# Scores of a token tile in two blocks, a new order of all queues and a paired maximum, in a six-layer windowed-attention kernel

## The reference

```python
x = attn_layer(shift_tokens(x), Wqkv[i], q_scale[i], k_scale[i], Wo[i]) + x
x = ffn_layer(shift_tokens(x), ln_g[i], ln_b[i], W1[i], b1[i], W2[i], b2[i]) + x
```

## Time and profile before

| | |
|---|---|
| median of 3 runs | 3304.71 us (3296.84 to 3305.41) |
| profiled execution | 3304.44 us, its span 3302.6 us |
| mean granted clock of TensorE | 0.991 of full |
| busy: PE, DVE, ACT, POOL | 94%, 85%, 83%, 78% |
| costliest group of DVE: sums of squares (L1153), 128x1024 to 16 | 384 of 1207 ns |
| DMA, mean | 68 GB/s |
| first output projection of a deep instance begins | 406 us |

### The profile page before, as it was taken

The page is one execution under the profiler, slowest core; times in us unless marked ns, Lnnn a source line. Parts: engine busy times, 40 slices in busy tenths (PEclk is TensorE's granted clock), DMA queues, the critical chain, the costliest instruction groups (busy, mean ns, idle before and its releaser), DMA issues.

```text
span 3302.6 us, 153819 instructions
## 1 busy us (share of the span) xinstructions
PE 3102.4 (94%) x65675; PEld 2395.8 (73%) x66148; DVE 2803.1 (85%) x4033; ACT 2755.6 (83%) x4817; POOL 2572.1 (78%) x2557
## 2 busy tenths in 40 slices
PE   8998789999999998999999999999999999999997
PEld 6886467777777776777777777777777777677776
DVE  6886788889988888889889888889998888888994
ACT  5665688889998888899888888889998888888886
POOL 3433887888888887888888888888888888788882
PEclk9999999999999999999999999999999999999999
DMA  1000222323332222233323223323332222322221
GB/s 46 29 3 32 72 64 75 83 61 77 78 81 68 77 75 63 74 78 76 78 66 83 70 61 77 79 62 83 78 78 71 74 74 58 93 70 59 71 75 52
DMA packets 140216, 224.66 MB, mean 68 GB/s; under 512 B 29456, under 2 KB 41360, under 8 KB 139152
## 3 DMA queue, kind: packets, MB, share of 16 engines
q1 hardware_dynamic: 139536, 214.78, 25.3%
HBM read 21.72 MB, written 4.19 MB: 8 GB/s over the span
## 4 chain that ended last, share of the span: by engine, by line
PE 85%; issue 6%; POOL 5%; DVE 2%; ACT 1%; POOLq 0%; DVEq 0%; ACTq 0%
PE bank L953 11%; PE bank L1019 11%; PE bank L1035 10%; PE bank L905 9%; PE bank L978 7%; PE bank L1365 7%; PE bank L906 7%; PE bank L997 5%; PE bank L904 4%; PE bank L1378 3%; PE bank L363 2%; PE bank L343 2%; PE bank L328 2%; POOL rotbuf L1282 1%; POOL rotbuf L1296 1%
## 5 line engine op out<-in xcount | busy, mean ns | idle before, releaser
L1282 POOL TENSOR_TENSOR rotbuf<-mbuf 128x512 f32<-128x512 f32 x768 | 975.8, 1276 | 311.0 <-PE bank L953 273.2
L1296 POOL TENSOR_TENSOR rotbuf<-rotbuf,rs 128x512 f32<-128x512 f32 x768 | 789.5, 1049 | 7.5
L1171 DVE TENSOR_TENSOR mbuf<-bank,table 128x512 f32<-128x512 f32 x768 | 523.3, 681 | 222.2 <-ACT sq L1061 189.5
L1172 DVE TENSOR_TENSOR mbuf<-bank,table 128x512 f32<-128x512 f32 x768 | 522.0, 680 | 0.0
L953 PE MATMUL bank<-ident,rotbuf 128*128 128x128 f32 x3072 | 471.4, 281 | 39.5 <-POOL rotbuf L1296 19.0
L1019 PEld LDWEIGHTS bank<-probs_t,vbuf 64*64 64x64 f32 x24576 | 393.3, 135 | 147.3 <-issue 147.3
L905 PE MATMUL bank<-weights,inputs 128*128 128x512 bf16 x1152 | 440.4, 382 | 38.0 <-issue 17.2
L1306 POOL TENSOR_TENSOR probs<-probs,rden 128x1024 f32<-128x1024 f32 x192 | 365.2, 1902 | 139.4 <-DVE rden L1248 139.3
L1061 ACT ACTIVATE sq<-bank 128x512 f32<-128x512 f32 x768 | 446.2, 595 | 27.9 <-PE bank L906 18.3
L1153 DVE TENSOR_REDUCE ss<-sq 128x16 f32<-128x1024 f32 x384 | 463.6, 1207 | 0.0
L906 PE MATMUL bank<-weights,inputs 128*128 128x512 bf16 x1152 | 440.0, 382 | 1.1 <-issue 1.1
(11 more groups left out here) (118 smaller groups left out, 5774.8 us busy)
## 6 DMA issues: line engine op xcount, KB each, us to landing
vbuf<-v_stage SPq DMA_DIRECT2D x1152, 128.0 KB
vbuf<-v_stage SPq DMA_DIRECT2D x576, 64.0 KB
stage<-in_wqkv SPq DMA_DIRECT2D x36, 256.0 KB, 2.8
weights<-in_wo SPq DMA_DIRECT2D x6, 512.0 KB, 4.7
...
```

The lines of the kernel that those rows point to most:

```text
L1171: e.tensor_tensor(b.m1[:, u % 2, :].rearrange("p (h s d) -> p h s d", h=8, s=2), pj, cos, ALU.mult)
L1172: e.tensor_tensor(b.m2[:, u % 2, :].rearrange("p (h s d) -> p h s d", h=8, s=2), pj[:, :, ::-1, :], sin, ALU.mult).then_inc(s.pj_free, 1)
L1282: e.tensor_tensor(b.rot[:, u, :], b.m1[:, u % 2, :], b.m2[:, u % 2, :], ALU.add).then_inc(s.rotated, 1)
L1296: e.tensor_tensor(v, v, r, ALU.mult).then_inc(s.scaled, 1)
```

## The change

Scores of a token tile come in two calls of 64 matmuls (i = 0 to 3: tile, half of the slots), with a finer count of `scores` and of the copies that they need. The calls of PE, ACT, DVE and POOL are listed in another order, the ring with them, and ACT and POOL work one instance less far behind. The clamp becomes a maximum over pairs, whose second element is a constant 1e-24. The layer norm's seed is written to the "mu" bank, not to ff_w, and the bank is released by `ff_rooted` (L1467). wo, w1 and w2 are loaded at three different sequences, and the attention weights' loads begin two sequences later.

```diff
 WORK_RING = (
-    ("pj", 6, 2), ("t", 5, 1), ("v", 0, 2), ("pj", 7, 2), ("up", 1, -2), ("up", 2, -2), ("t", 6, 1),
-    ("t", 7, 1), ("pj", 0, 3), ("mu", 0, -1), ("v", 1, 2), ("dn", 0, -2), ("t", 0, 2), ("v", 2, 2),
-    ("t", 1, 2), ("pj", 1, 3), ("pj", 2, 3), ("pj", 3, 3), ("t", 2, 2), ("v", 3, 2), ("t", 3, 2),
-    ("pj", 4, 3), ("t", 4, 2), ("out", 0, 0), ("pj", 5, 3), ("up", 0, -1),
+    ("t", 6, 1), ("t", 7, 1), ("pj", 0, 3), ("v", 1, 2), ("mu", 0, -1), ("pj", 1, 3), ("dn", 0, -2),
+    ("t", 0, 2), ("t", 1, 2), ("v", 2, 2), ("pj", 2, 3), ("v", 3, 2), ("t", 2, 2), ("t", 3, 2),
+    ("pj", 3, 3), ("pj", 4, 3), ("out", 0, 0), ("v", 0, 3), ("t", 4, 2), ("pj", 5, 3), ("up", 0, -1),
+    ("t", 5, 2), ("up", 1, -1), ("pj", 6, 3), ("up", 2, -1), ("pj", 7, 3),
 )
 PE_REACH = (-2, 3)
-ACT_REACH = (-3, 2)
+ACT_REACH = (-2, 3)
 DVE_REACH = (-5, 3)
-POOL_REACH = (-2, 3)
+POOL_REACH = (-1, 3)
 SP_REACH = (1, 3)
...
-STAGE_FROM, SPLIT_FROM, LATE_AT, OUTER_AT = 0, 3, 11, 4
+STAGE_FROM, SPLIT_FROM, OUTER_AT = 2, 3, 4
+LATE_AT = {9: 0, 11: 1, 13: 2}
...
             elif user == "mu":
-                e.wait_ge(s.ff_weighed, c[1] + 1)
+                e.wait_ge(s.ff_rooted, c[1] + 1)
...
-def pe_scores_of(e, s, b, at, ahead, t):
-    k = at(ahead)
-    if not k.ok:
-        return
+def pe_scores_of(e, s, b, at, ahead, i):
+    k = at(ahead)
+    if not k.ok:
+        return
+    t, half = divmod(i, 2)
     e.wait_ge(s.masked, k.c[STEPS] + (t + 1))
-    e.wait_ge(s.t_copied, k.c[8] + (4 * t + 4))
-    for slot in range(SLOTS):
+    e.wait_ge(s.t_copied, k.c[8] + (4 * t + 3 + half))
+    for slot in range(4 * half, 4 * half + 4):
...
-    if isq and half == 0:
-        e.wait_ge(s.scores, k.c[STEPS] + (t + 1 - STEPS))
-    if u == 0:
-        e.wait_ge(s.scores, k.c[STEPS] - STEPS)
+    if isq:
+        e.wait_ge(s.scores, k.c[SUBS] + (2 * t + half + 1 - SUBS))
+    elif t == 0:
+        e.wait_ge(s.scores, k.c[SUBS] + (half + 3 - 2 * SUBS))
...
-    e.tensor_reduce(b.ss[:, col:col + 16], sq, AX_X, ALU.add).then_inc(s.sq_summed, 1)
+    e.tensor_reduce(b.ss[:, col:col + 16, 0], sq, AX_X, ALU.add).then_inc(s.sq_summed, 1)
...
-    e.tensor_scalar(b.nx[:, :], b.ss[:, :], 1e-24, None, ALU.max).then_inc(s.clamped, 1)
+    e.tensor_reduce(b.nx[:, :], b.ss[:, :, :], AX_X, ALU.max).then_inc(s.clamped, 1)
...
-    e.wait_ge(s.scores, k.c[STEPS] + (t + 1))
+    e.wait_ge(s.scores, k.c[SUBS] + (2 * t + 2))
...
-    e.activation(w, w, ACT.Exp, bias=b.ff_consts[:, 1:2], scale=-0.5).then_inc(s.ff_seeded, 1)
+    seed = work_bank(b, k, "mu", 0)[:, 0:N_TOK]
+    e.activation(seed, w, ACT.Exp, bias=b.ff_consts[:, 1:2], scale=-0.5).then_inc(s.ff_seeded, 1)
     e.wait_ge(s.ff_seeded, k.c[1] + 1)
-    e.activation(b.ff_sq[:, :], w, ACT.Square, scale=2.0).then_inc(s.ff_squared, 1)
+    e.activation(b.ff_sq[:, :], seed, ACT.Square, scale=2.0).then_inc(s.ff_squared, 1)
...
-    e.scalar_tensor_tensor(w, a, 3.0, w, ALU.subtract, ALU.mult).then_inc(s.ff_rooted, 1)
+    e.scalar_tensor_tensor(w, a, 3.0, work_bank(b, k, "mu", 0)[:, 0:N_TOK], ALU.subtract, ALU.mult).then_inc(s.ff_rooted, 1)
...
-def sp_late_weights(e, s, b, layer):
+def sp_late_weights(e, s, b, layer, part):
 
 
     if layer > 1:
         e.wait_ge(s.ff_down, FIRST_N + (layer - 1) * SEQS)
-    e.dma_start(b.wo[layer % 2], b.wo_in[layer, :, :].rearrange("(c p) d -> p c d", p=P)).then_inc(s.wo_loaded, 16)
-    e.dma_start(b.w1[layer % 2], b.w1_in[layer, :, :]).then_inc(s.ff_loaded, 16)
-    e.dma_start(b.w2[layer % 2], b.w2_in[layer, :, :].rearrange("(c p) d -> p c d", p=P)).then_inc(s.ff_loaded, 16)
+    if part == 0:
+        e.dma_start(b.wo[layer % 2], b.wo_in[layer, :, :].rearrange("(c p) d -> p c d", p=P)).then_inc(s.wo_loaded, 16)
+    elif part == 1:
+        e.dma_start(b.w1[layer % 2], b.w1_in[layer, :, :]).then_inc(s.ff_loaded, 16)
+    else:
+        e.dma_start(b.w2[layer % 2], b.w2_in[layer, :, :].rearrange("(c p) d -> p c d", p=P)).then_inc(s.ff_loaded, 16)
...
-        if k.seq == LATE_AT:
-            sp_late_weights(e, s, b, k.layer + 1)
+        if k.seq in LATE_AT:
+            sp_late_weights(e, s, b, k.layer + 1, LATE_AT[k.seq])
...
-        b.ss, b.rs = sb("ss", [P, 4 * HEADS]), sb("rs", [P, 4 * HEADS])
+        b.ss, b.rs = sb("ss", [P, 4 * HEADS, 2]), sb("rs", [P, 4 * HEADS])
...
+                dve.memset(b.ss[:, :, 1:2], 1e-24)
```

The slots, as the calls in their order, before (-) and after (+). The prefix of the engine and the arguments `e, s, b` are left out: `scores_of(1, 2)` is `pe_scores_of(e, s, b, at, 1, 2)`, the instance one ahead, part 2. PE:

```diff
-project_in(2, 6), values_of(0, 0), transpose(1, 5), values_in(2, 0), transpose_probs_of(0, 2),
-project_in(2, 7), ff_up(-2, 1), ff_up(-2, 2), values_of(0, 1), transpose(1, 6), transpose(1, 7),
-project_in(3, 0), ff_mean(-1), scores_of(1, 0), values_in(2, 1), transpose_probs_of(0, 3),
-ff_variance(-1), ff_down(-2), values_of(0, 2), transpose(2, 0), values_in(2, 2), transpose(2, 1),
-project_in(3, 1), project_in(3, 2), project_in(3, 3), values_of(0, 3), scores_of(1, 1), transpose(2,
-2), values_in(2, 3), transpose_probs_of(1, 0), transpose(2, 3), project_in(3, 4), transpose(2, 4),
-project_out(0), project_in(3, 5), ff_up(-1, 0), transpose_probs_of(1, 1)
+transpose(1, 6), transpose(1, 7), project_in(3, 0), transpose_probs_of(0, 2), values_in(2, 1),
+ff_mean(-1), scores_of(1, 1), transpose_probs_of(0, 3), project_in(3, 1), ff_variance(-1),
+values_of(0, 2), values_of(0, 3), ff_down(-2), transpose(2, 0), transpose(2, 1), values_in(2, 2),
+project_in(3, 2), scores_of(1, 2), scores_of(1, 3), values_in(2, 3), transpose(2, 2), transpose(2,
+3), project_in(3, 3), project_in(3, 4), project_out(0), transpose_probs_of(1, 0), values_in(3, 0),
+transpose(2, 4), project_in(3, 5), ff_up(-1, 0), transpose_probs_of(1, 1), transpose(2, 5),
+scores_of(2, 0), ff_up(-1, 1), project_in(3, 6), ff_up(-1, 2), project_in(3, 7), values_of(1, 0),
+values_of(1, 1)
```

ACT:

```diff
-ff_square(-3), copy_out(-2, 0), copy_v(0, 1), ff_seed(-3), copy_pt_of(-2, 3), exp_of(-1, 0),
-copy_t(0, 0), copy_v(0, 2), copy_t(0, 1), square(1, 1), mask(-1, 1), square(1, 2), square(1, 3),
-copy_out(-2, 1), copy_t(0, 2), copy_v(0, 3), copy_t(0, 3), square(1, 4), copy_pt_of(-1, 0),
-input_of(2), ff_affine(-3), copy_t(0, 4), exp_of(-1, 1), mask(0, 0), square(1, 5), ff_gelu(-3, 0),
-square(1, 6), copy_pt_of(-1, 1), copy_t(0, 5), copy_v(1, 0), copy_pt_of(-1, 2), square(1, 7),
-ff_shift(-2), ff_gelu(-3, 1), ff_gelu(-3, 2), copy_t(0, 6), copy_t(0, 7), square(2, 0), seed(1)
+copy_t(1, 1), copy_v(1, 2), square(2, 2), copy_out(-1, 1), copy_v(1, 3), copy_t(1, 2), copy_t(1, 3),
+square(2, 3), square(2, 4), input_of(3), ff_affine(-2), exp_of(0, 1), mask(1, 0), copy_pt_of(0, 0),
+copy_v(2, 0), copy_t(1, 4), square(2, 5), ff_gelu(-2, 0), copy_t(1, 5), ff_gelu(-2, 1),
+copy_pt_of(0, 1), square(2, 6), ff_shift(-1), square(2, 7), ff_gelu(-2, 2), copy_t(1, 6), copy_t(1,
+7), square(3, 0), copy_pt_of(0, 2), seed(2), copy_out(0, 0), ff_square(-1), copy_pt_of(0, 3),
+square(3, 1), copy_v(2, 1), ff_seed(-1), mask(1, 1), exp_of(1, 0), copy_t(2, 0)
```

DVE:

```diff
-ff_refine(-2), sum_of(0, 0), rope(2, 1), rope(2, 2), rope(2, 3), sum_squares(2, 0), max_of(0, 1),
-shift(0, 1), rope(2, 4), sum_squares(2, 1), residual_of(-1), sum_of(0, 1), rope(2, 5), ff_gate(-2,
-0), rope(2, 6), sum_squares(2, 2), rope(2, 7), ff_gate(-2, 1), ff_gate(-2, 2), sum_squares(2, 3),
-clamp(2), ff_centre(-1), rope(3, 0), max_of(1, 0), shift(1, 0), ff_residual(-2), outer(-5)
+sum_squares(2, 2), rope(2, 6), ff_gate(-2, 2), rope(2, 7), sum_squares(2, 3), clamp(2), rope(3, 0),
+ff_centre(-1), max_of(1, 0), shift(1, 0), rope(3, 1), ff_refine(-1), ff_residual(-2), outer(-5),
+sum_of(1, 0), rope(3, 2), sum_squares(3, 0), max_of(1, 1), shift(1, 1), rope(3, 3), rope(3, 4),
+residual_of(0), sum_squares(3, 1), sum_of(1, 1), rope(3, 5), ff_gate(-1, 0), ff_gate(-1, 1)
```

POOL:

```diff
-rotate(1, 7), next_weights(at 1), refine(1), scale(1, 0), scale(1, 1), scale(1, 2), rotate(2, 0),
-normalise_of(0, 0), rotate(2, 1), scale(1, 3), scale(1, 4), rotate(2, 2), ff_norm(-2), rotate(2, 3),
-scale(1, 5), scale(1, 6), rotate(2, 4), normalise_of(0, 1), rotate(2, 5), scale(1, 7), input_of(3),
-rotate(2, 6)
+input_of(3), rotate(2, 5), scale(1, 7), normalise_of(0, 1), rotate(2, 6), rotate(2, 7),
+next_weights(at 2), refine(2), scale(2, 0), scale(2, 1), scale(2, 2), rotate(3, 0), scale(2, 3),
+scale(2, 4), rotate(3, 1), rotate(3, 2), ff_norm(-1), normalise_of(1, 0), scale(2, 5), scale(2, 6),
+rotate(3, 3), rotate(3, 4)
```

More of the change, by code:

```diff
@@ L767, in pe_deep_credit @@
     e.sem_inc(s.v_full, FIRST_N * 4)
-    e.sem_inc(s.scores, FIRST_N * STEPS)
+    e.sem_inc(s.scores, FIRST_N * SUBS)
     e.sem_inc(s.pt_full, FIRST_N * SUBS)
@@ L1726, in pool_deep_slot @@
+    dve_rope(e, s, b, at, 3, 2)
+    dve_sum_squares(e, s, b, at, 3, 0)
+    dve_max_of(e, s, b, at, 1, 1)
+    dve_shift(e, s, b, at, 1, 1)
+    dve_rope(e, s, b, at, 3, 3)
+    dve_rope(e, s, b, at, 3, 4)
+    dve_residual_of(e, s, b, at, 0)
+    dve_sum_squares(e, s, b, at, 3, 1)
+    dve_sum_of(e, s, b, at, 1, 1)
+    dve_rope(e, s, b, at, 3, 5)
+    dve_ff_gate(e, s, b, at, -1, 0)
+    dve_ff_gate(e, s, b, at, -1, 1)
+def pool_deep_slot(e, s, b, at):
+    pool_input_of(e, s, b, at, 3)
```

(10 more changed lines are left out.)

176 lines of the change are left out of this document (79 added, 97 removed).

## The result

| | before | after |
|---|---|---|
| median, us | 3305.06 | 3281.79 (4 runs, 3276.49 to 3284.19) |
| ratio | | 0.994, 95% interval 0.9926 to 0.9954 |
| profiled execution, its span | (above) | 3280.19, 3278.2 |
| mean granted clock | 0.991 | 0.993 |

The changed kernel is 23 us faster. The forecast was 74 us; the range (3195 to 3288) holds the time, the forecast's own range (3205 to 3255) doesn't.

A forecast was written before the change was run, and what follows sets the result against it. PE was taken to bound the kernel, losing 123 us, mostly to stalls for instructions; -58 - 12 - 9 + 5 = -74 us on 3304.4 gave 3230 us, own range 3205 to 3255, range 3195 to 3288.

The forecast's parts named there:

- The rival that the scores themselves stall: Stalls come from the scores (small loads, a bank), not the instruction stream; 64 + 64 pairs still stall; 3288 us, chance 0.09.
- Part 1: Scores in four blocks and a new PE order cut instruction stalls from 81 to 23 us; gain 58, bounds 20 and 81.
- the other score step: PE's 128 score pairs standing alone, 1.5 us; reckoned to stall 46 x 0.9 / 256 = 0.16 us per slot.
- the 3.3 us: Time the next block of 256 PE instructions takes to come: about 1.5 us of pairs plus 1.8 us mean idle.
- pairs of value steps: Two runs of 128 value pairs in PE's new order, 2.1 us; stalls of 2 x (32 x 0.6 / 256 = 0.075) us per slot.
- run of 192 pairs: PE's 64 value and 128 score pairs together in the old order; reckoned to stall 0.95 us per slot.
- Floor: PE's slot without waits, 29.10 us, stays; switches between 64-row and full matmuls, about 0.15 us each, stay five.
- Part 2: POOL's new order lets weight splits no longer delay the scale PE's transposition waits for; gain 12 us, bounds 0 and 13.
- Part 3: DVE's last-layer outer sum moves behind ff_refine, which releases the bank for transposition 0; gain 9 us, bounds 5 and 12.
- Part 4: Bank "mu" held one DVE instruction longer, until ff_rooted, and other near hand-offs; cost 5 us, bounds 0 and 40.
- Part 5: DVE's clamp as a paired maximum takes 0.15 to 0.4 us, not 0.936; its path has cover, so 0 gain.
- 6 (weights, 0): Late weights in three parts, stage loads two slots later on SP's queue, same bytes; 0, bounds -3 and +3.

The follow-up runs named there:

- e2_pad: Changed kernel with 64 tiny matmuls once ahead of the loop, shifting later block ends by 128 instructions; 3269.64 us in one run.
- e7: Changed kernel with 12 implied waits left out (1280-instruction slot) and 64 tiny matmuls ahead, every block end in sparse work; 3189.58 us, ratio 0.9645.
- e10: Kernel before with 10 implied waits left out (1280-instruction slot) and no matmuls ahead, block ends held in values and scores; 3375.05 us.
- e3_outer: Kernel before with DVE's outer sum of the last layer moved behind ff_refine, one instance later; 3303.49 us in one run.

## Why the prediction was right in kind and wrong in size

**What bounds the kernel: right.** PE bounds it, the stalls are ends of 256-instruction blocks. When PE's loads, matmuls and wait instructions are counted from the first on, all 963 gaps of over 0.2 us inside the runs of scores and values, of all 18 traces, lie at position 192 or 193 modulo 256, and none elsewhere; shifting the count moves them by slots (e2_pad), holding it still removes or fixes them (e7, e10). The rival that the scores themselves stall had 3288 us, 6 us beside the result, and is still wrong: without a block end in them, the same scores run without a stall.

**Part 1 (-58 us): this step failed.** The slip is in the sentence "the other score step (128 pairs in 1.5 us, alone) gives 46 x 0.9 / 256 = 0.16" and in the 3.3 us on which it rests. The 3.3 us were taken as counted from the last block's end: a run of 128 pairs that PE entered with sparse work behind it would thus nearly always find its block on the way. The trace shows a fetch that doesn't start at the block end but with the run (0 to 0.9 us after its start), even where the block end lay 90 instructions, some 4 us, ahead. What the run then finds is 2.5 us of fetch against 1.0 to 1.5 us of pairs. So the pair of score blocks stalls at pairs 83 to 127, 90 instructions of 256 and not 46, for 1.8 us and not 0.9: 59 / 92 = 0.64 us per slot instead of 0.16. The pairs of value steps stall mostly at pairs 102 to 127, for 0.9: 22 / 92 = 0.24 instead of 0.15. In all 81 us where 23 were forecast. The trace of before had the warning: its lone score step cost 22 us in 18 stalls, where 0.16 x 92 x 0.8 = 12 were reckoned; its run of 192 pairs cost 66 where 0.95 x 92 x 0.8 = 70 were. The prediction did note that each scores call has two conditions, "which costs a wait instruction", and reckoned that only as two more instructions per slot. That was the costly one: with it out, the changed kernel takes 3211 to 3214 us, a little below the forecast of 3230.

The Trainium skill, page Runtime: NRT & Kernel Launch, section Instruction fetch mechanics, has the crossing of a block "mostly hidden". No more than the trace of before do these runs agree: 81 us of 3280 aren't hidden, and 136.6 + 95 x 0.2 = 156 us of the 3375 in e10. Where the block ends fall in sparse work, it holds (e7).

**Floor (0 us): missed, +15 us.** "The number of switches stays five" is true and was not enough. Up behind scores and down behind values cost 0.2 and 0.18 us more than in the places that the chain has for them otherwise. That the 0.16 per slot come from there is likely, not shown: other places got cheaper, and no run takes them apart.

**Part 2 (POOL, -12): right in its mechanism, half in size.** The waits of L954 for POOL fell from 12.4 to 1.5 us, but 31 short ones of 4.9 us in all stand at L906 in their place: 6 us net. **Part 3 (outer sum, -9): right.** The 9.3 us of waits for ff_sq are gone, and in e3_outer eight slots take 1.0 us less by this part alone.

**Part 4 (bank "mu", +5): 0.** No wait for L1470 is in the table; L1470 itself is 0.16 us shorter than the L1467 of the earlier trace rows, which the prediction took over unchanged, and that is more than the 0.05 feared.

**Part 5 (clamp, 0) and 6 (weights, 0):** nothing speaks against either, but no run takes one alone. The clamp's 0.286 us lies in the 0.15 to 0.4 given. Advanced Engine Details and Errata of the Trainium skill, section VectorE Performance Modes, would have had POOL gain with it. From 1000 to 2000 us POOL's two large groups (L1284, L1298) were at 1276 and 1051 ns before and are at 1272 and 1042 now, and its busy time from 2572.1 to 2562.8 us, 0.1 us per clamp against the 0.65 that DVE gained; so the larger part of DVE's gain didn't come out of POOL.

**The start and the end**, 7.3 and 4 us, weren't in the sum. The sum as measured on spans: stalls 0, floor +15, POOL -6, outer sum -9, start -7, end -4, and some -12 of small waits and single events make -24 (with the fractions left off here), the difference of the two spans. What the -12 are was not followed up.

What stays open: why a second wait ahead of a dense run delays the fetch by more than 1 us, why it did so in only half of the stalls of the lone score step before, and whether the same holds ahead of the values, whose first step carries three. The runs show only that it does so at the scores of the changed kernel.
